# Two attention layers on one core: both projection halves first, then eight transposes, then the output projection

## What is computed

```python
def layer0(x, adj):                       # edge attributes are adj itself
    nx = ln(x, ln1_g, ln1_b)
    q, k, v = heads(nx @ wq + bq), heads(nx @ wk + bk), heads(nx @ wv + bv)
    scores = q @ k.T / sqrt(32) + where(adj > 0, 0.1 * adj * adj, -inf)
    x1 = x + (softmax(scores) @ v) @ wo + bo
    return x1 + gelu(ln(x1, ln2_g, ln2_b) @ w1 + b1) @ w2 + b2

def layer1(x, adj):
    q, k, v = heads(x @ Wq + bq), heads(x @ Wk + bk), heads(x @ Wv + bv)
    scores = where(adj == 0, -inf, q @ k.T / sqrt(32))
    y = (softmax(scores) @ v) @ Wo + bo + x
    return ln(y, gamma, beta)
```

## Time and profile before

| | |
|---|---|
| median of 3 runs | 2176.55 us (2176.46 to 2181.41) |
| the profiled execution | 2176.37 us |
| its span, first to last instruction | 2174.5 us |
| TensorE matmuls busy | 2140.2 us (98%), 20372 instructions |
| TensorE weight loads busy | 1854.5 us (85%) |
| VectorE busy | 1801.7 us (83%) |
| ScalarE busy | 1684.7 us (77%) |
| GpSimd busy | 1154.6 us (53%) |
| mean granted TensorE clock | 0.996 |
| chain that ended last | TensorE 96%, VectorE 2%, ScalarE 1% |

### The profile page before, as it was taken

The page is one execution under the profiler, slowest core; times in us unless marked ns, Lnnn a source line. Parts: engine busy times, 40 slices in busy tenths (PEclk is TensorE's granted clock), DMA queues, the critical chain, the costliest instruction groups (busy, mean ns, idle before and its releaser), DMA issues.

```text
span 2174.5 us, 59064 instructions
## 1 busy us (share of the span) xinstructions
PE 2140.2 (98%) x20372; PEld 1854.5 (85%) x20372; DVE 1801.7 (83%) x8415; ACT 1684.7 (77%) x5658; POOL 1154.6 (53%) x1264
## 2 busy tenths in 40 slices
PE   8899999999999999999999999999999999999997
PEld 6888888888888888888888888888888888888876
DVE  6788888888888888888888888888888888888885
ACT  5677887778787778777787877787877788777875
POOL 4445555545655445655455554456554455554554
PEclk9999999999999999999999999999999999999998
DMA  4100111010111011111101110101110011101000
GB/s 129 33 31 28 38 33 40 29 32 29 40 33 40 24 33 34 38 35 31 33 26 41 33 40 26 35 28 40 34 40 23 28 38 34 39 31 31 19 26 18
DMA packets 94309, 75.76 MB, mean 35 GB/s; under 512 B 8128, under 2 KB 93760, under 8 KB 94016
## 3 DMA queue, kind: packets, MB, share of 16 engines
q1 hardware_dynamic: 94016, 71.99, 10.8%
HBM read 55.20 MB, written 16.78 MB: 33 GB/s over the span
## 4 chain that ended last, share of the span: by engine, by line
PE 96%; DVE 2%; ACT 1%; issue 1%; POOL 0%; DMA 0%; SPq 0%; POOLq 0%; DVEq 0%; ACTq 0%
PE p_bank L1233 67%; PE p_heads L1367 10%; PE p_heads L1354 8%; PE p_bank L1386 7%; PE p_bank L1266 4%; ACT scores L692 1%; DVE probs_t L999 0%; DVE scores L925 0%; DVE normed L952 0%; PE p_bank L1156 0%; DMA scores<-in_L_gnn_wk 0%; DVE x_two L832 0%; SPq L469 0%; DVE normed L946 0%; PE p_heads L1156 0%
## 5 line engine op out<-in xcount | busy, mean ns | idle before, releaser
L692 ACT ACTIVATE scores<-scores,negmax 128x128 f32<-128x128 f32 x2048 | 793.8, 393 | 22.7 <-DVE negmax L925 22.3
L615 POOL TENSOR_TENSOR scores<-scores,inverse 128x512 f32<-128x512 f32 x512 | 542.0, 1064 | 324.9 <-DVE inverse L936 324.9
L692 ACT ACTIVATION_READ_ACCUMULATOR scores<-scores,negmax 128x1 f32 x2048 | 392.1, 191 | 0.0
L1233 PEld LDWEIGHTS p_bank<-w_down,hidden 128*128 128x128 f32 x3072 | 374.6, 190 | 8.5 <-issue 5.9
L1233 PE MATMUL p_bank<-w_down,hidden 128*128 128x256 f32 x3072 | 381.8, 284 | 0.0
L1233 PE MATMUL p_bank<-normed,w_up 128*128 128x512 f32 (+1 forms) x1584 | 369.3, 389 | 3.6 <-DVE normed L946 2.9
L1233 PEld LDWEIGHTS p_bank<-normed,w_up 128*128 128x128 f32 x1584 | 286.2, 188 | 67.0 <-issue 10.2
L1367 PE MATMUL p_heads<-ident,scores 128*128 128x128 f32 x2048 | 310.0, 274 | 7.0 <-DVE negmax L925 4.4
L925 DVE CUSTOM_DVE_ANT_0 scores<-p_heads,adj_a 128x128 f32<-128x128 f32 x1024 | 235.1, 285 | 43.8 <-issue 43.7
L1367 PEld LDWEIGHTS p_heads<-ident,scores 128*128 128x128 f32 x2048 | 239.3, 140 | 32.9 <-DVE negmax L925 12.4
L735 ACT ACTIVATE p_bank<-p_bank,ready_cols 128x512 f32<-128x512 f32 x248 | 164.2, 662 | 126.8 <-PE p_bank L1233 121.5
(11 more groups left out here) (130 smaller groups left out, 3709.8 us busy)
## 6 DMA issues: line engine op xcount, KB each, us to landing
res_a<-in_x SPq DMA_DIRECT2D x32, 512.0 KB, 3.8
out<-res_c SPq DMA_DIRECT2D x128, 128.0 KB, 1.7
x_in<-in_x SPq DMA_DIRECT2D x31, 512.0 KB, 3.9
adj_a<-in_adj SPq DMA_DIRECT2D x32, 256.0 KB, 2.9
adj_c<-in_adj SPq DMA_DIRECT2D x32, 256.0 KB, 2.8
piece_room<-in_L_gnn_w SPq DMA_DIRECT2D x2, 512.0 KB, 9.0
x_two<-in_x SPq DMA_DIRECT2D x1, 512.0 KB, 6.2
res_c<-in_L_gnn_w SPq DMA_DIRECT2D x1, 512.0 KB, 7.0
```

What stands on the lines that cost most here:

```text
L615: nc.gpsimd.tensor_tensor(rows_g, rows_g, inverse[:, step % 2, heads].unsqueeze(2).broadcast_to([P, HC, P]), ALU.mult).then_inc(probs_made, 1)
L692: last = nc.scalar.activation(scores[:, k % 2, h], scores[:, k % 2, h], ACT.Exp, scale=-1.0, bias=negmax[:, k % 2, h:h + 1], accum_out=tot ...
L1233: last = nc.tensor.matmul(dst, stationary(i), moving(j), start=(n == 0), stop=(n == total_n - 1))
```

## The change

In the turns that have a turn before them, except the last two, the steps 0, 1, 3, 4, 5 and 6 are `joined`. At 0, 1, 5 and 6 the second half of the projection moves from `fill` to `mid`, so that it is issued behind the first half, ahead of the transposes. At all six, T1 is issued right behind T0, ahead of W, and VectorE's copy of T1 stands ahead of `add_residual` instead of behind it. ScalarE's lists follow the tables: it evacuates both halves, then copies T0. The numbering of the banks follows too (W is the fourth use of its step, not the third).

```diff
+        self.joined = [0, 1, 3, 4, 5, 6] if before is not None and it not in (NG, NG + 1) else []
+        for k in self.joined:
+            if k not in (3, 4) and k in self.fill:
+                self.mid[k] = self.mid.get(k, []) + self.fill.pop(k)
...
+                    if k in s.joined:
+                        for _, r in only("T", lag):
+                            turned(t, r)
                     for _, r in only("W", lag):
                         add_residual(t, r)
-                    for _, r in only("T", lag):
-                        turned(t, r)
+                    if k not in s.joined:
+                        for _, r in only("T", lag):
+                            turned(t, r)
...
                     for _, r in only("T", lag):
                         turn(t, r, 0)
+                        if k in s.joined:
+                            turn(t, r, 1)
                     for op, r in only("W", lag):
                         lagging(t, op, r)
                     for _, r in only("T", lag):
-                        turn(t, r, 1)
+                        if k not in s.joined:
+                            turn(t, r, 1)
```

## The result

The changed kernel takes 2200.82 us (median of 4 runs, 2199.89 to 2205.69) against 2178.17 (median of 4, 2176.46 to 2181.41) for the kernel before. The ratio on record is 1.0108, 95% interval 1.0094 to 1.0122; the two medians alone stand at 1.0104. It is slower by 1.1%. The prediction said 2201.1, which is within 0.4 us of the median; that closeness is partly luck, as is worked out further down. The profiled execution takes 2200.47 us, its span is 2198.6; before it was 2176.37 and 2174.5.

The account below looks back on a forecast made before the run. TensorE was taken as the bound, the joined steps newly waiting for VectorE's copy: 3 x 0.23 + 0.12 = 0.81 us per turn, 23.5 over 29 turns, 24.7 with turn 1, on 2176.37: 2201.1 us, range 2193 to 2212.

Parts of the forecast that it names:

- The bound and the cover: Loop: TensorE is the bound; the projection's second half hides VectorE's copy of the second transposes, with 0.60 us to spare.
- The constant from step 4: Second transpose group's start to next scores, read in step 4: 0.60 + 0.04 + 0.69 + 0.15 = 1.48 us, for every joined step.
- Joined steps: Steps 0, 1 and 6 of each turn: +0.23 us each, 6.04 us against 5.81 in step 6.
- the second half in a run: Projection's second half issued straight after the first in joined steps: 1.39 us on TensorE.
- the seams: Switches between kinds of TensorE blocks that the change removes: worth zero, with 0.02 us per step either way.
- Steps 4 and 5: Scores of step 5 start sooner, then that step gets longer: together +0.12 us per turn, bounds +0.01 and +0.19.
- Step 3: Output projection and second transposes swap ahead of six up-projections, which hide the copy: zero, at most +0.09 us.
- steps 2 and 7: The steps of each turn that are not joined: no change, zero.
- turn 1: The turn before the loop, joining steps 5 and 6 as well: +0.95 us in step 5, +0.23 in step 6.
- The wait stays hidden: Rival: copy ready when the output projection ends in the four joined steps; -0.11 us per turn, 2174 us; 7%.
- VectorE late as well: Rival: VectorE's later work delays step 2's mask and uses up its slack, a longer normalisation giving 2218 us; 8%.
- The clock: Rival: new gaps make TensorE's granted clock fall for one stretch in every turn, 49 us, 2250 us; 2%.

Follow-up runs that it names:

- e2: Changed kernel with both projection halves first, but the two transpose groups again around the output projection and VectorE's old order: 2289.59 us (one run).
- e6: Changed kernel with the copy of the second transpose group shared between VectorE and ScalarE, a bank each, ScalarE evacuating the second half afterwards: 2175.64 us, 0.998.
- e1: Changed kernel with the projection's second half put back behind the output projection; transposes still joined, VectorE's new order kept: 2196.12 us, 1.0078.
- e8: Changed kernel with two needless 128 x 256 additions on VectorE at the end of step 1 in 29 turns: 2216.62 us, 1.0167.
- e10: e1 with step 5 left unjoined, as in the kernel before: 2194.43 us, 1.0067.
- e5: Changed kernel with VectorE copying the second transpose group bank by bank, the first bank once its two transposes are done: 2182.41 us, 1.0011.
- e3: Changed kernel with VectorE's old order, the residual addition ahead of the copy of the second transpose group: 2338.83 us (one run).
- e7: Changed kernel meant to get one needless VectorE addition, which was never in the program; the changed kernel again on another chip: 2203.08 us, 1.0113.

## Why the prediction was right

**The bound and the cover** were read rightly. The earlier trace rows show the copy hidden behind the second half, with 0.60 us to spare; the change takes that cover, and the trace after shows the wait where it was said to be, 126 times ("some 120"), T1 to scores 1.475 us ("1.47 to 1.48"), clock 1.00.

**The constant from step 4** carried the forecast. The earlier trace rows gave 0.60 + 0.04 + 0.69 + 0.15; after the change the same four terms are 0.60, 0.04, 0.69 and 0.14, and e2 has 1.48 with an idle TensorE. An operation of the same size whose wait is visible elsewhere in the trace was the right place to read it from.

**Joined steps: +0.205 to +0.211, predicted +0.23.** The term that was too large is the second half in a run: 1.39 us was taken from the earlier trace rows, and in step 6 it costs 2.867 - 1.502 = 1.365. The others held: 1.23, 1.50, 0.44 and 1.48 against 1.231, 1.502, 0.436 and 1.475. The 1.39 was a misreading as well. That row of the chain is no group in a run: it is the second half of step 5 of the kernel before, which stands behind T1, and the chain counts it from T1's modelled end (884.66 + 0.65) to its own (885.07 + 1.64). Two groups in a run do stand in that trace, in step 3:

```profile
884.66 0.65 PE L1367 MATMUL p_heads<-ident,scores 128*128 128x128 f32 x4
885.07 1.64 PE L1233 MATMUL p_bank<-normed,w_k 128*128 128x512 f32 x6
...
918.57 3.03 PE L1233 MATMUL p_bank<-normed,w_up 128*128 128x512 f32 x12
921.43 0.60 PE L1367 MATMUL p_heads<-ident,scores 128*128 128x128 f32 x4
```

Twelve products take 921.43 - 918.57 = 2.86 us up to the transposes there, so the second six take 1.36. That the misread figure came within 0.03 us of it is luck. The 0.03 is also what the seams give back, as e6's 5.77 us shows from the other side; the prediction took zero for them, with 0.02 either way.

**Steps 4 and 5: +0.10, predicted +0.12.** Step 5's scores start 0.067 us sooner and no longer wait, as said; its scores to first half take 0.017 longer since the split of x follows only by 0.05 (0.07 was taken).

**Step 3: -0.01; steps 2 and 7: +0.018 and +0.015, both predicted 0.** The two unjoined steps follow a later VectorE. Together the turn is +0.743 in place of +0.81, and no term of a joined step came out the other way.

**Two counts were wrong, and they cancel.** The text on the kernel before says that turns 2 to 30 are a loop of 29 passes. No turn is marked as a loop; all 34 are written out, and turn 31 has the same eight steps and is joined too: 30 equal turns, 30 x 0.743 = 22.3 us. And turn 1 was given +0.95 us in step 5 and +0.23 in step 6. It gained 0.18 and 0.22, with 0.04 in step 7: +0.44. The sum compared only what follows T1 (0.35 + 1.57 us before), but this step has no W, and already in the kernel before it has the wait that e1 met:

```profile
90.16 0.60 PE L1367 MATMUL p_heads<-ident,scores 128*128 128x128 f32 x4
91.31 0.63 PE L1367 MATMUL p_heads<-ident,scores 128*128 128x128 f32 x4 [0.55 <-DVE negmax L925]
```

T1 follows T0 by 1.15 us, where 0.44 would do, because it waits for the masks; the change puts the second half ahead of it and takes that wait away. So the trace of the kernel before already showed what joining the transposes alone would cost.

22.3 + 0.4 is 22.7 of the 24.1 us that the span grew by. Of the remaining 1.4, 1.1 lies at the very end, where no step is joined: from the last but one of the 256 scores to the end it is 23.30 us before and 24.41 after (columns as in the earlier trace rows):

```profile
2151.25:2174.55 23.30, 12.85 (x144) 9.94 (x144) 14.05 (x73) 9.72 (x42) 11.90 (x15) 0.75 0.07 24
2174.24:2198.65 24.41, 14.25 (x144) 10.88 (x144) 14.11 (x73) 9.65 (x42) 11.84 (x15) 0.71 0.07 22
```

TensorE works little more than half of this time. The same 144 matmuls keep it busy 1.40 us longer, at a mean granted clock of 0.71 in place of 0.75, a mix of 2.4 and 1.2 GHz. In e1 the stretch takes 21.72 us, 10.79 of them busy, at 0.92; in e6 and e8, which keep the new order, it takes 23.29 and 23.30 as in the kernel before. So this part goes with the clock that was granted in one execution or the other, not with the order of the blocks.

Against the sum of 24.7 us the turn brings -1.9 (29 turns of 0.07), the thirtieth turn +0.7, turn 1 -0.7 and the rest +1.4: together about the 24.1 measured. Besides, the forecast started from 2176.37, and the median of the kernel before, with a fourth run, is 2178.17: the medians differ by 22.65 us. To come within 0.4 us was luck; what the reasoning earned is 0.743 of 0.81 us per turn.

**The rivals.** *The wait stays hidden* was priced at -0.11 us per turn, 2174 us. e6, which hides it, has -0.12 and 2175.64, and 1.238 us from T1 to the scores where 1.25 was taken: the sum was right, but its condition (T1 to the copy's end plus 0.15 under 1.25) isn't met by one copy of 0.69 us. *VectorE late as well* did not decide. VectorE in the change, end of step 1 and step 2, beside the earlier trace rows, with TensorE's scores and T1 of step 2:

```profile
853.57 0.42 DVE L1020 TENSOR_TENSOR res_a<-p_bank,res_a 128x256 f32<-128x256 f32 x1
853.70 0.73 PE L1363 MATMUL p_heads<-keys_c,queries_c 32*128 32x128 f32 x16 [0.17 <-DVE probs_t L1004]
854.03 0.43 DVE L823 BATCH_NORM_STATS2 stats_M<-res_a 128x6 f32<-128x256 f32 x1
...
855.13 0.28 DVE L930 CUSTOM_DVE_ANT_0 scores<-p_heads,adj_c 128x128 f32<-128x128 f32 x1
...
857.02 0.28 DVE L930 CUSTOM_DVE_ANT_0 scores<-p_heads,adj_c 128x128 f32<-128x128 f32 x1
...
857.57 0.60 PE L1376 MATMUL p_heads<-ident,scores 128*128 128x128 f32 x4
```

The masks start 1.43 us after the scores, where 1.51 was worked out and 0.80 was the case before: the mechanism is there. TensorE can see their end at 857.30 + 0.15 = 857.45, and T1 starts at 857.57, so 0.12 us is left; the prediction said none. e8 shows the price beyond that point. *The clock* stayed at 1.00 in the turn with eight transposes ahead of each gap. The Trainium skill, "TensorE: Matmul & The Clock Gate", Part 4 (PE-mode transpose), says that transposes do not count as PE-busy in the same way; the trace after shows no effect of that here, with 1.00 in every turn of the steady part.

**What the prediction didn't see** is e1's and e10's result. It treated joining the transposes as a change of T1's successor only. Bringing T1 forward also brings forward its need for the masks and the scaled probabilities. In the change itself this costs nothing in the equal turns, because the second half moves ahead of it, so the forecast didn't suffer; a forecast for half of the change would have been wrong by some 17 us (0.78% of 2178, e1).

## What to carry to other kernels

Work that is issued between a producer and the consumer of its copy is cover, and moving it elsewhere is paid as soon as the copy chain (here 1.47 us: transposes, handover, one copy of a bank pair, handover) is longer than what still stands there. Before giving cover away, shorten the chain: two engines with a bank each took the same order of blocks from 1.011 of the time before to 0.998. And a moved block has two sides: ask who now reads its result sooner, and also whether its inputs are ready sooner; both halves of this change alone lose, by opposite shortages.

## What the runs showed that was not expected

- Four transposes to the scores that need their copy: 1.475 us in the change and 1.472 to 1.474 in steps 0, 1, 5 and 6 of e2, whether TensorE does W's six matmuls in between or nothing.
- A copy of 128 x 512 float32 out of PSUM takes 0.69 us on VectorE and 0.58 to 0.60 on ScalarE; of 128 x 256, 0.42 and 0.38. On VectorE the second of two such halves starts 0.34 us after the first (831.27 and 831.61 in e5), so both take 0.75 us together, 0.06 more than one copy.
- A mere change of place between two short VectorE operations (e3) moved the time by 136 us against the changed kernel on the same chip (2203.08, e7), six times what the change that was studied did.
